# A graph network's edge loop: twelve groups of edges gathered by TensorE instead of seven, in a PSUM bank of their own, and two of VectorE's one-hot builds merged

## The chip, the cores and the metric

One NeuronCore of a Trainium2 chip. The metric is the device time of one launch in microseconds. Before the change it is 1136.53 us, the median of three runs (1135.17 to 1138.17).

## The reference

3125 nodes with 128 features, 100000 edges sorted by destination, float32. Two graph layers, each followed by a residual sum and a layer norm:

```python
# layer 0, on x
msgs = z[edge_dst] @ Wd + z[edge_src] @ Ws + edge_weight[:, None] * ww[None, :] + bm
agg = segment_max(msgs, edge_dst)            # 0 for nodes without an edge
out = relu(z @ W1a + agg @ W1b + b1) @ W2 + b2
x = layernorm(x + out)
# layer 1, on x, twice (128 -> 256 with relu, 256 -> 128)
mean = segment_sum(x[src], dst) / max(deg, 1)
h = mean @ Wl.T + bl + x @ Wr.T
x = layernorm(x + h2)
```

The term `z[edge_src] @ Ws` is a gather of rows from the table zs = x @ Ws, which is written to memory once (`zs_d`).

## The kernel before

**Groups and slots.** The edges are cut into 196 groups of 512 (two superbatches of 256). All engines step through the same numbered slots k, each with its own order written out by hand in a loop `for k in range(SLOTS)`, and meet by semaphores. In slot k, TensorE (PE) first does the halves of `pieces` that fall there, then `rows_T(k)` (the messages of group k, transposed into `T_BANK`: one matmul for the edge weights, L1614, and four transposes of gathered rows, L1626), `adjacent(k-2)` (L1675, L1678: counts of edges per source tile and destination column; L1685: the running maxima at the ends of segments), `products(k-1)` (four transposes of the scan, L1665), the matmuls of a node tile if one is due, `degree`, and last the `pick_rows` of this slot. VectorE (DVE) does `scan(k)` (L1225), `pick(k-1)` (L1217), `one_hots(k-1)` (L1208 to L1210), the steps of a node tile, degree rows and their reciprocal (L1244, L1249), and `make_hot` for the next slot (L1303). ScalarE (ACT) does `cast_hot` (L909), `adjacent` (L863, L864: counts copied into `adj`, maxima into `aggT`), `messages` (L869) and copies for the node tiles. SyncE (SP) loads the mask row and the weights of group k (`load_edges`, L502, L505), stores tiles and scale rows, and loads `parts_d` quads; its queue is in order, and it waits on semaphores in it.

**Gathers.** GpSimd (POOL) issues four indirect DMAs for each group (L1037), 128 rows of 128 floats each, into the ring `gring`, which has places for GR = 4 groups. For group g it waits until `rows_T(g-4)` is done (`t_ps`). Five groups (`OWN`: 38, 70, 102, 134, 166) take their last 128 rows by plain DMAs of SP, so POOL has three gathers there.

**Picked groups.** POOL skips the groups in `PICKED`. Their rows are gathered by PE: for each of the 25 node tiles, `make_hot` on DVE compares 512 source numbers with the tile's 128 node numbers (128x512, float16 in, bfloat16 out), `cast_hot` on ACT turns that into fp32r, and `pick_rows` multiplies it by the high and the low half of the table's tile (two matmuls with 512 columns, L1785). `PICKS` pairs each picked group with the slot at which this begins: (17, 7), (28, 17), (37, 28), (48, 37), (60, 50), (80, 71), (93, 85). The 25 tiles are spread evenly over those slots (`hots`). The sums are kept in `L_BANK` until `rows_T` of that group adds the edge weights.

**What else is in L_BANK.** The first layer-1 sums (`pieces`, L1748, planned by `plan()`: from slot 49 on, 12 matmuls with 512 columns over two slots each, then more of them) and the degree rows (`degree`, L1706, slots 61 to 65, 93 to 97, 125 to 129 and later). So picks are placed between them, and each waits for the other with `scanned(picked_before(...))` and `acc_sb`, `deg_sb`.

**Node tiles.** Tile t (128 nodes) is complete at slot `turn(t)` = 8t + 9. Its x is transposed into bank `M1` at slot turn + 1, `values` follows at + 3, `hidden` (DVE, L1258) at + 4, `outputs` at + 5, `stats`, root and `normed` at + 6 to + 8, and `roots` and `copy_zr` at + 12 and + 13.

After the loop (from about 981 us) follow the rest of layer 1 and the second aggregation as a product with the count matrix; the change does not touch them, but for the steps of the last two node tiles.

Of the kernel before, what the change touches and what calls it, by code (L numbers as in the profile page):

```python
# [4 lines left out]
P = 128  # L5
# [17 lines left out]
HR = 4  # L23
# [26 lines left out]
PICKS = ((17, 7), (28, 17), (37, 28), (48, 37), (60, 50), (80, 71), (93, 85))  # L50
# [3 lines left out]
HOTS = 4  # L54
ROW = AW // 2
SPARE = 801
# [70 lines left out]


def picked_before(k):
    return max([g for g in PICKED if g < k], default=-1)  # L130
# [10 lines left out]
def gnn_kernel(nc, x, src, dst, w, Wm, bm, W1, b1, W2, b2, W1lT, b1l, W1rT, W2lT, b2l, W2rT, out):  # L141
# [19 lines left out]
    with ctx:  # L161
# [69 lines left out]
        def spare(row, n, lead=0):  # L231
            return slice(row * ROW + SPARE + lead, row * ROW + SPARE + lead + n)

        key_i = adj_w[:, spare(0, 512)].bitcast(i32)
        key_w = adj_w[:, spare(1, 512)]
        keys = [adj_w[:, spare(2, 256, 256 * i)].bitcast(f16) for i in range(2)]
        hot_b = [adj_w[:, spare(3 + i // 2, 256, 256 * (i % 2))].bitcast(bf16) for i in range(HOTS)]
        hot_r = [nc.alloc_sbuf_tensor_at(f"hot_r{i}", [P, 512], f32r, offset=adj_at + 32 * ((ROW * (5 + i) + SPARE) // 8))[:, :]
                 for i in range(HOTS)]

# [13 lines left out]
        raw_l = raw_w.rearrange("p (a b) -> p a b", b=512)  # L254
        quads = quad, raw_w[:, 0:6 * F].bitcast(bf16).rearrange("p (a b) -> p a b", b=3 * F)
# [79 lines left out]
        T_BANK, S_BANK, L_BANK, A_BANK, M0, M1 = bank[0:2], bank[2], bank[3], bank[4:6], bank[6], bank[7]  # L335
# [113 lines left out]
        def _(sp):  # L449
# [65 lines left out]
            def usual():  # L515
# [47 lines left out]
                def load_key(i):  # L563
                    g = PICKED[i]
                    if i:
                        sp.wait_ge(key_float, i)
                    sp.dma_start(key_i, src[512 * g:512 * g + 512].rearrange("(o e) -> o e", o=1).broadcast_to([P, 512])).then_inc(l_key, 16)
# [214 lines left out]
        def _(act):  # L782
# [67 lines left out]
            def usual():  # L850
# [20 lines left out]
                def copy_xr(t):  # L871
                    act.wait_ge(xr_ps, t + 1)
                    if t:
                        act.wait_ge(v_ps, t)
                    nc.scalar.copy(xTt[:, 0:size(t)], M1[:, P:P + size(t)]).then_inc(xr_sb, 1)
# [10 lines left out]

                def copy_zr(t):
                    act.wait_ge(zr_ps, t + 1)
                    for a in range(2):
                        last = nc.scalar.activation(zr_of(t)[:, a, 0:size(t)], M1[:, (2 + a) * P:(2 + a) * P + size(t)], ACT.Identity, bias=b1l_c[:, a:a + 1])  # L890
                    last.then_inc(zr_sb, 1)
# [6 lines left out]
                def key_to_float(i):  # L898
                    act.wait_ge(l_key, 16 * (i + 1))
                    if i:  # L900
                        act.wait_ge(keyed, i)
                    nc.scalar.copy(key_w, key_i).then_inc(key_float, 1)

                def cast_hot(i, h):
# [4 lines left out]
                    nc.scalar.copy(hot_r[u % HOTS], hot_b[u % HOTS]).then_inc(hot_cast, 1)  # L909

                for k in range(SLOTS):
# [14 lines left out]
                    for t in tiles(k, 13, -1):  # L926
                        copy_zr(t)
                    for t in tiles(k, 10):
                        copy_x1T(t)
                    for t in tiles(k, 7):  # L930
# [171 lines left out]
        def _(dve):  # L1102
# [98 lines left out]
            def usual():  # L1201
                def one_hots(g):
                    for s in supers(g):
                        if s >= HR:
                            dve.wait_ge(ae_ps, s - HR + 2)
                        r = s % HR
                        for u in range(2):
                            nc.vector.tensor_scalar(hot_l[:, r, u, :], i_key[:, 0:P], lo_n[:, u, s:s + 1], None, ALU.is_equal)  # L1208
                            nc.vector.tensor_scalar(hot_d[:, r, u, :], i_key[:, 0:COLS], key_n[:, u, s:s + 1], None, ALU.is_equal)  # L1209
                        nc.vector.tensor_scalar(hot_x[:, r, 0:NT], i_hi[:, 0:NT], key2_n[:, s:s + 1], None, ALU.is_equal).then_inc(made, 1)  # L1210
# [8 lines left out]
                def scan(g):  # L1219
# [5 lines left out]
                    nc.vector.tensor_tensor_scan(S[:, g % 2, 0:n], mask[:, g % MR, 0:n], (L_BANK if g in PICKED else T_BANK[g % 2])[:, 0:n],  # L1225
# [24 lines left out]

                def hidden(t):
                    k = size(t)
                    dve.wait_ge(v_ps, t + 1)
                    if 0 < t < NT - 1:
                        dve.wait_ge(x1_st, 32 * t)
                        dve.wait_ge(parts_sb, t)
                        dve.wait_ge(x1T_sb, t)
                    nc.vector.tensor_scalar(hid(t)[:, 0:k], M0[:, 0:k], c0_c, 0.0, ALU.add, ALU.max).then_inc(hid_sb, 1)  # L1258
# [35 lines left out]
                def key_of(i):  # L1294
                    dve.wait_ge(key_float, i + 1)
                    nc.vector.tensor_scalar(keys[i % 2], key_w, float(CENTER), None, ALU.subtract).then_inc(keyed, 1)

                def make_hot(i, h):
                    u = NT * i + h
                    dve.wait_ge(keyed, i + 1)  # L1300
                    if u >= HOTS:
                        dve.wait_ge(hot_cast, u - HOTS + 1)
                    nc.vector.tensor_scalar(hot_b[u % HOTS], keys[i % 2], node_c[:, h:h + 1], None, ALU.is_equal).then_inc(hot_made, 1)  # L1303

                for k in range(SLOTS):
# [14 lines left out]
                    for t in tiles(k, 4):  # L1320
                        hidden(t)
# [234 lines left out]
        def _(pe):  # L1556
# [51 lines left out]
            def rows_T(g):  # L1608
                n, o = edges(g), T_BANK[g % 2]
                pe.wait_ge(l_wp[g % WR], 16 * (g // WR + 1))  # L1610
                if g in PICKED:
                    nc.tensor.matmul(L_BANK[:, :], ww9[0:9, :], wp9[:, g % WR, 0:n], start=False, stop=True).then_inc(t_ps, 1)
# [47 lines left out]
            def usual():  # L1660
# [29 lines left out]
                def x_turned(t):  # L1690
# [4 lines left out]
                    if t >= 2:  # L1695
                        pe.wait_ge(zr_sb, t - 1)
# [299 lines left out]
```

## Time and profile before

| | before |
|---|---|
| median of 3 runs | 1136.53 us |
| profiled execution, its own time | 1136.4 us |
| its span | 1134.6 us |
| PE busy | 997.1 us (88%) |
| DVE busy | 894.9 us (79%) |
| ACT busy | 500.8 us (44%) |
| POOL busy | 757.0 us (67%) |
| mean granted TensorE clock | 0.958 |

Busy time counts each instruction's record from its start to its end. Records of neighbouring instructions on PE and DVE overlap, since these engines are pipelined: what an instruction costs its engine is the distance from its start to the next one's start, which is shorter than its record.

### The profile page before, as it was taken

What the parts mean: (1) busy time and instruction counts of PE and PEld (TensorE: products, weight loads), DVE (VectorE), ACT (ScalarE), POOL (GpSimd) and SP (SyncE); (2) the same over time, 40 slices, a digit from 0 to 9 for tenths busy, and PEclk for the clock granted to TensorE, in tenths of its full rate; (3) what the DMA queues carried; (4) which work ended last, traced back from release to release, by engine and by line L of the source; (5) the groups of instructions that cost most, each with busy time, mean ns of one, the idle gap of its engine ahead of it and who ended that gap; (6) DMA issues with size and microseconds to landing.
All of it is one profiled execution on the core that took longest, in us unless ns stands there. A gap on an engine that the chain in (4) does not pass through costs nothing.

```text
span 1134.6 us, 23462 instructions
## 1 busy us (share of the span) xinstructions
PE 997.1 (88%) x6407; PEld 735.8 (65%) x6449; DVE 894.9 (79%) x3127; ACT 500.8 (44%) x1434; POOL 757.0 (67%) x802
## 2 busy tenths in 40 slices
PE   4689999999997999978797879886889899899997
PEld 4367767767765777756665656565556577656776
DVE  6488999999886999897777778777788788746455
ACT  3256766666542656533333323333324233312664
POOL 6657777777777777777777777777777777200332
PEclk9789999999997999989898889999999999999999
DMA  8724344344344343334434334433344354446221
GB/s 210 214 61 94 92 98 109 94 99 114 89 97 106 91 119 97 91 85 127 110 87 93 90 97 129 105 91 89 87 132 110 106 150 97 117 134 177 83 58 42
DMA packets 123128, 121.14 MB, mean 107 GB/s; under 512 B 24307, under 2 KB 106392, under 8 KB 122989
## 3 DMA queue, kind: packets, MB, share of 16 engines
q1 hardware_dynamic: 95920, 69.21, 22.7%
q0 software_dynamic: 23968, 49.13, 18.0%
q10 hardware_dynamic: 3101, 1.21, 0.4%
q8 instruction: 54, 0.88, 0.3%
q14 instruction: 85, 0.70, 0.2%
HBM read 105.60 MB, written 13.88 MB: 105 GB/s over the span
## 4 chain that ended last, share of the span: by engine, by line
PE 36%; POOL 30%; issue 15%; DVE 12%; DMA 3%; SPq 2%; ACT 1%; ACTq 1%; DVEq 0%
POOL area L1037 30%; PE bank L1910 7%; PE bank L1748 5%; PE bank L1685 5%; PE bank L1675 3%; PE bank L1626 3%; PE bank L1785 3%; DVE area L1225 2%; DVE area L1209 2%; PE bank L1665 2%; PE bank L1875 2%; DVE area L1208 2%; PE bank L1614 2%; PE bank L1861 1%; PE bank L1706 1%
## 5 line engine op out<-in xcount | busy, mean ns | idle before, releaser
L1037 POOL DMA_INDIRECT area<-zs_d,area x729 | 705.4, 968 | 234.8 <-issue 219.3
L863 ACT CAST adj_w<-bank 128x325 f32 x391 | 176.2, 451 | 472.5 <-PE bank L1685 415.1
L1225 DVE TENSOR_TENSOR_SCAN area<-area,bank 128x512 f32<-128x512 bf16 x196 | 249.7, 1274 | 144.1 <-PE bank L1626 126.5
L1209 DVE TENSOR_SCALAR area<-area 128x325 bf16<-128x325 f16 x782 | 249.5, 319 | 0.0
L1685 PE MATMUL bank<-area 128*128 128x104 f32 x1564 | 234.0, 294 | 0.1
L1208 DVE TENSOR_SCALAR area<-area 128x128 bf16<-128x128 f16 x782 | 212.1, 271 | 0.0
L1685 PEld LDWEIGHTS bank<-area 128*128 128x128 f32 x1564 | 204.7, 204 | 11.3 <-ACT area L869 1.9
L1675 PE MATMUL bank<-area 128*128 128x325 bf16 x782 | 157.2, 316 | 22.0 <-DVE area L1210 15.8
L1626 PE MATMUL bank<-ident,area 128*128 128x128 f32 x734 | 123.1, 291 | 45.8 <-DMA area<-zs_d,area 45.4
L1626 PEld LDWEIGHTS bank<-ident,area 128*128 128x128 f32 x734 | 78.1, 142 | 91.1 <-DMA area<-zs_d,area 57.2
L1748 PE MATMUL bank<-adj_w,area 128*128 128x512 bf16 (+5 forms) x497 | 108.5, 357 | 24.6 <-DMA area<-parts_d 8.6
L1665 PE MATMUL bank<-ident,area 128*128 128x128 f32 x782 | 121.0, 278 | 0.0
L869 ACT COPY area<-bank 128x512 f32<-128x512 f32 x196 | 118.3, 604 | 4.7 <-issue 3.3
L909 ACT CAST hot_r<-adj_w 128x512 fp32r<-128x512 bf16 x175 | 98.0, 622 | 48.3 <-DVE adj_w L1303 47.5
L1058 POOL CAST counts<-adj_w 128x512 fp32r<-128x512 bf16 (+2 forms) x45 | 28.2, 631 | 124.1 <-DVE area L1357 74.7
L1785 PE MATMUL bank<-hot_r,zs_r 128*128 128x512 f32 (+1 forms) x350 | 99.7, 414 | 0.4 <-issue 0.3
L1210 DVE TENSOR_SCALAR area<-area 128x25 bf16<-128x25 bf16 x391 | 97.4, 249 | 0.0
L1665 PEld LDWEIGHTS bank<-ident,area 128*128 128x128 f32 x782 | 96.1, 151 | 0.3 <-issue 0.3
L1614 PE MATMUL bank<-area,ww 9*128 9x512 bf16 x189 | 74.4, 394 | 20.9 <-DMA area<-wp_d 20.8
L1675 PEld LDWEIGHTS bank<-area 128*128 128x128 bf16 x782 | 61.6, 100 | 45.9 <-DVE area L1210 22.9
L1748 PEld LDWEIGHTS bank<-adj_w,area 128*128 128x128 bf16 (+1 forms) x525 | 48.6, 98 | 64.3 <-issue 21.4
L1678 PE MATMUL bank<-area 128*128 128x25 bf16 x390 | 74.5, 191 | 0.0
(174 smaller groups left out, 1067.6 us busy)
## 6 DMA issues: line engine op xcount, KB each, us to landing
area<-mask_d SPq DMA_DIRECT2D x195, 128.0 KB
area<-zs_d,area POOLq DMA_INDIRECT x729
area<-zs_d SPq DMA_DIRECT2D x640, 0.5 KB
area<-parts_d SPq DMA_DIRECT2D x20, 384.0 KB, 7.6
area<-wp_d SPq DMA_DIRECT2D x195, 9.0 KB
zr_d<-area SPq DMA_DIRECT2D x24, 128.0 KB
area<-zr_d SPq DMA_DIRECT2D x6, 512.0 KB, 4.5
area<-scale_d SPq DMA_DIRECT2D x11, 256.0 KB, 4.3
```

What stands on the lines that cost most here:

```text
L863: nc.scalar.copy(adj[:, :, bass.ds(at, W)], A_BANK[s % 2][:, 0:COLS].rearrange("p (h w) -> p h w", w=W))
L869: nc.scalar.copy(St[:, 0:n], S_BANK[:, 0:n]).then_inc(st_sb, 1)
L1037: pool.indirect_dma_start(gring[:, g % GR * 4 + s % 2 * 2 + u, :], None, x if g < RAW else zs_d[0:N, :], bass.IndirectOffsetOnAxis(ap=firs ...
L1208: nc.vector.tensor_scalar(hot_l[:, r, u, :], i_key[:, 0:P], lo_n[:, u, s:s + 1], None, ALU.is_equal)
L1209: nc.vector.tensor_scalar(hot_d[:, r, u, :], i_key[:, 0:COLS], key_n[:, u, s:s + 1], None, ALU.is_equal)
L1225: nc.vector.tensor_tensor_scan(S[:, g % 2, 0:n], mask[:, g % MR, 0:n], (L_BANK if g in PICKED else T_BANK[g % 2])[:, 0:n], S[:, (g + 1) % ...
L1626: last = nc.tensor.matmul(o[:, b * P:(b + 1) * P], rows, ident[:, :], start=False, stop=b == n // P - 1, is_transpose=True)
L1665: last = nc.tensor.transpose(S_BANK[:, b * P:(b + 1) * P], S[:, g % 2, b * P:(b + 1) * P], ident[:, :])
L1675: last = nc.tensor.matmul(o[:, 0:COLS], hot_l[:, r, u, :], hot_d[:, r, u, :], start=u == 0, stop=u == 1 and s == 0)
L1685: last = nc.tensor.matmul(o[:, 384:384 + WIDE * W].rearrange("p (n w) -> p n w", w=W), St[:, b * P:(b + 1) * P], sel[:, g % 2, u, s % 2, : ...
L1748: last = nc.tensor.matmul(o[:, 0:b - a], row[0:k, i * F:(i + 1) * F], adj[0:k, h, a:b], start=start and i == 0, stop=stop and i == 2)
L1785: last = nc.tensor.matmul(L_BANK[:, :], part_of[0:n, h - SPLITS[at][1], :], hot_r[u % HOTS][0:n, :], start=h == 0 and part_of is zs_high[a ...
```

## The change

`PICKS` becomes twelve groups over slots 20 to 145, end to end. They get bank 7 (`G_BANK`) for themselves, and the waits between picks, pieces and degrees go. The node tiles' x and root products move from that bank into `M0`, `roots` and `copy_zr` come a slot earlier, and `hidden` moves from DVE to ACT (`hidden_of`). On DVE, the four 128x128 one-hots of a group become one `tensor_tensor` and the two 128x25 ones another. The buffers of the picks move (`hot_r`, the keys: four runs of 128 words in rows of `adj`, `hot_b`: three buffers in `aggT`).

```diff
-PICKS = ((17, 7), (28, 17), (37, 28), (48, 37), (60, 50), (80, 71), (93, 85))
+PICKS = ((30, 20), (40, 30), (51, 40), (61, 51), (72, 61), (82, 72), (93, 82), (103, 93), (114, 103), (124, 114), (135, 124),
+         (145, 135))
...
-        hot_b = [adj_w[:, spare(3 + i // 2, 256, 256 * (i % 2))].bitcast(bf16) for i in range(HOTS)]
+        hot_r = [nc.alloc_sbuf_tensor_at(f"hot_r{i}", [P, 4 * ROW], f32r, offset=adj_at + 32 * ((ROW * (8 + 4 * i) + SPARE) // 8))[:, :]
+                 .rearrange("p (h n) -> p h n", n=ROW)[:, :, 0:P] for i in range(HOTS)]
+        hot_b = [aggT[:, FREE + 256 * i:FREE + 256 * i + 256].bitcast(bf16) for i in range(RAWS)]
...
+        def x_bank(t):
+            return (M0 if t < NT - 2 else G_BANK)[:, P:2 * P]
+        def root_bank(t):
+            return M0[:, P:3 * P] if t < NT - 2 else G_BANK[:, 2 * P:4 * P]
...
+                def hidden_of(t):
+                    k = size(t)
+                    act.wait_ge(v_ps, t + 1)
+                    if 0 < t < NT - 1:
+                        act.wait_ge(x1_st, 32 * t)
+                        act.wait_ge(parts_sb, t)
+                        act.wait_ge(x1T_sb, t)
+                    nc.scalar.activation(hid(t)[:, 0:k], M0[:, 0:k], ACT.Relu, bias=c0_c).then_inc(hid_sb, 1)
...
                 def one_hots(g):
-                    for s in supers(g):
-                        if s >= HR:
-                            dve.wait_ge(ae_ps, s - HR + 2)
-                        r = s % HR
-                        for u in range(2):
-                            nc.vector.tensor_scalar(hot_l[:, r, u, :], i_key[:, 0:P], lo_n[:, u, s:s + 1], None, ALU.is_equal)
-                            nc.vector.tensor_scalar(hot_d[:, r, u, :], i_key[:, 0:COLS], key_n[:, u, s:s + 1], None, ALU.is_equal)
-                        nc.vector.tensor_scalar(hot_x[:, r, 0:NT], i_hi[:, 0:NT], key2_n[:, s:s + 1], None, ALU.is_equal).then_inc(made, 1)
+                    s, m = 2 * g, len(supers(g))
+                    r = s % HR
+                    if s >= HR:
+                        dve.wait_ge(ae_ps, min(s + m, NS) - HR + 1)
+                    low = lo_n[:, :, s:s + m].unsqueeze(3).broadcast_to([P, 2, m, P])
+                    count = i_key[:, 0:P].unsqueeze(1).unsqueeze(1).broadcast_to([P, 2, m, P])
+                    nc.vector.tensor_tensor(hot_l[:, r:r + m, :, :].rearrange("p s u e -> p u s e"), count, low, ALU.is_equal)
+                    for n in range(m):
                         for u in range(2):
+                            nc.vector.tensor_scalar(hot_d[:, r + n, u, :], i_key[:, 0:COLS], key_n[:, u, s + n:s + n + 1], None, ALU.is_equal)
+                    carried = key2_n[:, s:s + m].unsqueeze(2).broadcast_to([P, m, NT])
+                    tiles_at = i_hi[:, 0:NT].unsqueeze(1).broadcast_to([P, m, NT])
+                    nc.vector.tensor_tensor(hot_x[:, r:r + m, 0:NT], tiles_at, carried, ALU.is_equal).then_inc(made, m)
...
                 def pick_rows(i, h):
                     u, n = NT * i + h, size(h)
                     if h == 0:
-                        g, a = PICKS[i]
                         pe.wait_ge(zs_low_sb, len(SPLITS))
-                        pe.wait_ge(raw_sb, RAW)
                         if i:
                             pe.wait_ge(scanned, PICKED[i - 1] + 1)
-                        before = len([p for p in PIECES if p[0] < a])
-                        if before:
-                            pe.wait_ge(acc_sb, before)
-                        rows = len([d for d in DEGREE_SLOTS if d < a])
-                        if rows:
-                            pe.wait_ge(deg_sb, rows)
                     pe.wait_ge(hot_cast, u + 1)
                     at = [b for b, (_, h0, h1) in enumerate(SPLITS) if h0 <= h < h1][0]
                     for part_of in (zs_high[at], zs_low[at]):
-                        last = nc.tensor.matmul(L_BANK[:, :], part_of[0:n, h - SPLITS[at][1], :], hot_r[u % HOTS][0:n, :],
+                        last = nc.tensor.matmul(G_BANK.rearrange("p (a e) -> p a e", e=P), part_of[0:n, h - SPLITS[at][1], :], hot_r[u % HOTS][0:n],
                                                 start=h == 0 and part_of is zs_high[at], stop=False)
                     last.then_inc(hot_used, 1)
```

## Rows read from the trace of the kernel before

**Rows 1.** The page: the chain that ended last, by engine and by line.
```profile
PE 36%; POOL 30%; issue 15%; DVE 12%; DMA 3%; SPq 2%; ACT 1%; ACTq 1%; DVEq 0%
```

**Rows 2.** Waits, whole span: who waited for whom, us in total, times, longest.
```profile
POOL area L1037 <- PE bank L1626: 14.6, 16, 8.6
```

**Rows 3.** POOL's groups of instructions: xcount | busy, mean ns | idle before; 170.8:259.9, then 727.8:816.5.
```profile
L1037 POOL DMA_INDIRECT area<-zs_d,area x69 | 68.6, 995 | 21.0 <-issue 20.1 <-PE bank L1626 0.9
...
L1037 POOL DMA_INDIRECT area<-zs_d,area x71 | 68.1, 959 | 21.6 <-issue 21.6
```

**Rows 4.** Waits of PE in 540:640, a stretch without picks.
```profile
PE bank L1626 <- DMA area<-zs_d,area: 16.6, 12, 2.4
```

**Rows 5.** Busy time by stretch: us, PE, PEld, DVE, ACT, POOL, PEclk, DMA share, GB/s.
```profile
76.60:259.90 183.30, 175.87 (x1186) 133.29 (x1185) 172.07 (x643) 122.62 (x330) 140.57 (x141) 0.99 0.40 98
```

**Rows 6.** The scans L1225 alone, by stretch (x50 is groups 0 to 49).
```profile
0.00:264.01 264.01, 62.43 (x50) 0.96 0.48 120
264.01:727.81 463.80, 122.61 (x96) 0.94 0.41 101
```

**Rows 7.** The gathers L1037 alone, up to the scan of group 49.
```profile
3.80:264.01 260.21, 189.27 (x188) 0.96 0.48 121
```

**Rows 8.** PE in order of time, one slot with picks: start, us, line, xcount.
```profile
250.68 0.38 PE L1614 MATMUL bank<-area,ww 9*128 9x512 bf16 x1
...
252.10 1.12 PE L1685 MATMUL bank<-area 128*128 128x104 f32 x8
...
253.49 0.39 PE L1725 MATMUL bank<-w,area 128*128 128x128 f32 x2
253.63 1.18 PE L1785 MATMUL bank<-hot_r,zs_r 128*128 128x512 f32 x4
254.75 0.39 PE L1614 MATMUL bank<-area,ww 9*128 9x512 bf16 x1
```

**Rows 9.** PE in order of time, stretches 136:138 and 351:372.
```profile
136.77 1.32 PE L1785 MATMUL bank<-hot_r,zs_r 128*128 128x512 f32 x5
...
351.94 0.38 PE L1614 MATMUL bank<-area,ww 9*128 9x512 bf16 x1 [2.13 <-DMA area<-wp_d]
...
364.58 2.34 PE L1748 MATMUL bank<-adj_w,area 128*128 128x512 bf16 x5 [4.22 <-DMA area<-parts_d]
...
371.15 1.46 PE L1748 MATMUL bank<-adj_w,area 128*128 128x512 bf16 x6
```

**Rows 10.** DVE in order of time, 251:255 and 345:349.
```profile
251.69 1.28 DVE L1225 TENSOR_TENSOR_SCAN area<-area,bank 128x512 f32<-128x512 bf16 x1
252.89 0.19 DVE L1217 TENSOR_TENSOR area<-area 128x52 f32<-128x52 bf16 x1
...
253.80 0.23 DVE L1210 TENSOR_SCALAR area<-area 128x25 bf16<-128x25 bf16 x1
253.94 0.24 DVE L1208 TENSOR_SCALAR area<-area 128x128 bf16<-128x128 f16 x1
254.10 0.30 DVE L1209 TENSOR_SCALAR area<-area 128x325 bf16<-128x325 f16 x1
...
345.20 3.34 DVE L1249 RECIPROCAL area<-area 1x512 f32<-1x512 f32 x1
```

**Rows 11.** Groups by shape: the nearest operations to the new ones.
```profile
L1394 DVE TENSOR_TENSOR area<-area 128x512 f32<-128x512 f32 x5 | 3.4, 684 | 2.4 <-DMA area<-r_d 2.4
...
L890 ACT ACTIVATE area<-bank,cols 128x128 f32<-128x128 f32 x48 | 15.6, 390 | 1.6 <-PE bank L1742 1.6
```

**Rows 12.** POOL and DVE in order of time, about 137.9 and about 201.7.
```profile
137.73 0.61 DVE L1303 TENSOR_SCALAR adj_w<-adj_w,node_c 128x512 bf16<-128x512 f16 x2
137.91 1.24 POOL L1037 DMA_INDIRECT area<-zs_d,area  x1 [0.30 <-issue]
...
201.57 0.94 POOL L1037 DMA_INDIRECT area<-zs_d,area  x1 [0.30 <-PE bank L1626]
...
201.96 0.29 DVE L1287 TENSOR_TENSOR area<-area 128x128 bf16<-128x128 f32 x1
```

More of the change, by code:

```diff
@@ L229, in gnn_kernel, with spare @@
         zs_low = [z[:, :, low_at:ROW] for z in zs_r]
[L231 to L236, printed above, removed]
-        hot_b = [adj_w[:, spare(3 + i // 2, 256, 256 * (i % 2))].bitcast(bf16) for i in range(HOTS)]
-        hot_r = [nc.alloc_sbuf_tensor_at(f"hot_r{i}", [P, 512], f32r, offset=adj_at + 32 * ((ROW * (5 + i) + SPARE) // 8))[:, :]
-                 for i in range(HOTS)]
+        def spare(row, rows):
+            return adj_w.rearrange("p (h n) -> p h n", n=ROW)[:, row:row + rows, SPARE:SPARE + P]
+        key_w = spare(0, 4)
+        key_i = key_w.bitcast(i32)
+        keys = [spare(4 + 2 * i, 2).bitcast(f16) for i in range(2)]
+        hot_r = [nc.alloc_sbuf_tensor_at(f"hot_r{i}", [P, 4 * ROW], f32r, offset=adj_at + 32 * ((ROW * (8 + 4 * i) + SPARE) // 8))[:, :]
+                 .rearrange("p (h n) -> p h n", n=ROW)[:, :, 0:P] for i in range(HOTS)]
         AREA = 15776
@@ L889, in copy_zr @@
                     for a in range(2):
-                        last = nc.scalar.activation(zr_of(t)[:, a, 0:size(t)], M1[:, (2 + a) * P:(2 + a) * P + size(t)], ACT.Identity, bias=b1l_c[:, a:a + 1])
+                        last = nc.scalar.activation(zr_of(t)[:, a, 0:size(t)], root_bank(t)[:, a * P:a * P + size(t)], ACT.Identity, bias=b1l_c[:, a:a + 1])
                     last.then_inc(zr_sb, 1)
@@ L925, in usual @@
                             key_to_float(i)
-                    for t in tiles(k, 13, -1):
+                    for t in tiles(k, 12):
                         copy_zr(t)
@@ L929, in usual @@
                         copy_x1T(t)
+                    for t in tiles(k, 4):
+                        hidden_of(t)
                     for t in tiles(k, 7):
@@ L1611, in rows_T @@
                 if g in PICKED:
[L1612 removed]
+                    nc.tensor.matmul(G_BANK[:, :], ww9[0:9, :], wp9[:, g % WR, 0:n], start=False, stop=True).then_inc(t_ps, 1)
                     return
@@ L1741, in roots @@
                     for a in range(2):
-                        last = nc.tensor.matmul(M1[:, (2 + a) * P:(2 + a) * P + k], w1r[:, a * P:(a + 1) * P], zr_of(t)[:, 0, 0:k], start=True, stop=True)
+                        last = nc.tensor.matmul(root_bank(t)[:, a * P:a * P + k], w1r[:, a * P:(a + 1) * P], zr_of(t)[:, 0, 0:k], start=True, stop=True)
                     last.then_inc(zr_ps, 1)
@@ L1821, in usual @@
                         products(k - 1)
-                    for t in tiles(k, 12, -1):
+                    for t in tiles(k, 11):
                         roots(t)
```

51 lines of the change are left out of this document (21 added, 30 removed).

## The prediction, written before the changed kernel was run

> **What bounds the kernel now.** I read the page first. Its chain splits the span between PE and POOL [rows 1]: neither view alone says what a change is worth. The waits come next: the pace of the loop is POOL's. POOL waited for PE 14.6 us in all, 8.6 of them at once in the start-up [rows 2]; otherwise it issued gather after gather, and what it sat idle before each is its own issue time of 0.3 us. So one gather costs (68.1 + 21.6)/71 = 1.26 us where nothing is picked, and (68.6 + 21.0)/69 = 1.30 us where picks run [rows 3]. In a stretch without picks PE waits for the rows to land [rows 4]. With four gathers a slot that is 5.04 us a slot, and a picked group costs POOL nothing.
>
> Where picks run it is different. From the scan of group 7 to that of group 48, 41 slots take 183.3 us, 4.47 a slot, with PE 175.9 us busy and DVE 172.1 [rows 5]. All three engines are near their end there. What the change is worth is therefore PE's work in the slots 49 to 145, where picks now run beside pieces and degrees.
>
> **What POOL is spared.** Twelve picked groups in place of seven: 5 x 4 = 20 gathers, at 1.26 to 1.30 us 25 to 26 us. No group of `OWN` is picked. If only POOL counted, that would be the gain.
>
> **What PE has to do in a slot.** A slot with two of the 25 node tiles of a pick goes from 250.68 to 254.75, 4.07 us [rows 8]. A matmul of a pick costs (1.32 - 0.41)/4 = 0.23 us from start to start (five in a run, the last counted with its record of about 0.41) [rows 9]. The two of L1725 go from 253.49 to 253.63, and by the next ones' distance I take 0.11 each for any 128-column float32 matmul of a node tile. So the bare slot is 4.07 - 4 x 0.23 - 2 x 0.11 = 2.93 us. A matmul of a piece costs (1.46 - 0.38)/5 = 0.216 [rows 9]; a degree's has the same shape.
>
> From slot 49 to slot 145 (96 slots) after the change, on PE:
> - 96 x 2.93 = 281.3
> - 12 node tiles x 12 small matmuls x 0.11 = 15.8
> - 230 pick tiles (50 + 77 + 75 + 28 by `hots`) x 2 x 0.232 = 106.7
> - 12 pieces x 12 x 0.216 = 31.1, and 75 degree matmuls x 0.216 = 16.2
> - less 9 picked groups x 4 transposes x 0.11 = -4.0
>
> Sum 447.1 us. POOL has 341 gathers in these slots, 430 to 443 us. So PE becomes the bound there, if narrowly.
>
> **What PE loses on top.** In rows 5 I can size what the sum leaves out: 41 x 2.93 + 100 x 0.464 + 5 x 1.32 - 4 x 0.44 = 171.4 of 183.3 us, 0.29 us a slot. There DVE was as full as PE, and a node tile's steps on DVE held PE up. After the change DVE has less in each slot. The merged 128x128 one-hots: the nearest rows are L1394, a tensor_tensor with 512 float32 elements, 0.684 us [rows 11], less the 0.08 by which a record overlaps the next start (the scan: 1.28 long, 1.20 to the next) [rows 10], 0.60 us, against 4 x 0.16 = 0.64 for the four. From below it could be no longer than one 128x325 instruction (0.3); from above 0.68; I take 0.60, since `lo_n` is float32 as in L1394. The merged 128x25 has 50 elements: at most the 0.16 of one L1208 with 128, against 2 x 0.14 for L1210 [rows 10]. `hidden` leaves too, 0.26 us in eight slots. Together 0.19 us a slot less, while PE's slot grows from 4.2 to 4.65; so DVE is no longer beside PE, and I take nothing for the steady slots. The new single wait of `one_hots` (for the first superbatch of group g-1 instead of the second one of g-2) costs nothing: PE's fourth L1685 of the slot ends at about 252.10 + 3 x 0.12 + 0.28 = 252.74 [rows 8], before DVE's pick has begun at 252.89 [rows 10]. Its price if PE is late: 0.5 us a slot for DVE, which has that.
>
> What does not go away is the three reciprocals of degree rows, 3.34 us each on DVE [rows 10], at slots 66, 98 and 130, now all in slots full of picks. The scan behind one is late by that, PE waits for it, and SP, which waits for the row too, loads the next weights late: the 2.13 us before L1614; the quad behind it costs 4.22 us more [rows 9]. Before, these waits fell where PE had 1 us to spare a slot. Now PE arrives later at each (1.1 us a slot), which hides most of the quad and the weights, but not the scan. I take 3.3 us each, 10 in all; bounds: 0, and 3 x (3.34 + 2.13 + 4.22) = 29.
>
> Does the merged instruction hold POOL up? A gather beside the picks' 128x512 one-hots lasts 1.24 us instead of 0.94, but one beside L1287, a tensor_tensor with both operands in SBUF, 0.94 [rows 12], so I take nothing for it. The Trainium skill ("SBUF — State Buffer", Who interferes with whom) speaks against the change here: a DVE instruction with two SBUF inputs contends with a GpSimd instruction that reads SBUF, and L1287 is four times shorter than the new one. By the row the sum stays; by the rule the merge has a price, which is rival 4.
>
> **The path.** At slot 49 there have been two picks instead of four by then: POOL is 8 gathers further back, 8 x 1.28 = 10.2 us. PE was behind POOL there: 188 gathers issued where 183 were needed [rows 7], 5 against 3 where POOL bounds, so 2.5 us are won back. Slot 49 comes at 264.0 + 7.7 = 271.7 us. Slot 145 comes at 271.7 + 447.1 + 10 = 728.8, against 727.8 before [rows 6]: no gain up to there. But POOL has run ahead meanwhile. The ring holds at most three groups and the one just freed, 12 gathers, or 8 where a picked group is among them, against 3 now: 5 to 9 gathers, 6 to 11 us; I take 9. PE can make it up in the 17 slots from 145 to 162, 17 x 3.1 + 48 x 0.216 + 25 x 0.216 = 68 us of work in 88.7 us (727.8 to 816.5) [rows 3]. From 162 on nothing changes. The gain is 9 - 1 = 8 us. Against the profiled execution, 1136.4 us (its span 1134.6 and 1.8 around it; the median is 1136.5), that gives 1128.4.
>
> The smaller edits: `hidden_of` puts a 0.39 us activation on ACT [rows 11] every eighth slot, where ACT is busy 122.6 of 183.3 us [rows 5]; if ACT were full it would cost 25 x 0.39 = 10 us. The picks read in four runs of 128 cost PE nothing: L1685 reads runs of 13 without showing it. If each run went like a matmul of its own (0.11), 230 x 2 x 0.21 = 97 us would come on top; I hold that end for unlikely. The tail after 981 us keeps its order; `hidden` on ACT there costs 0.05 us a tile.
>
> **The rivals.**
> 1. POOL stays the bound everywhere (chance 0.15). For it: PE's sum is only 4 to 17 us over POOL's, and the ring covers 9 of that. Against it: the reciprocals. Then the 20 gathers count in full, less 125 more pick tiles that stretch some gathers: 17 to 25 us, 1115.
> 2. The gain is eaten up (0.16): PE loses 0.18 us a slot more than I take and the result is within 0.3% (3.4 us), 1136. I call 0.3% what this kernel's measurement can just tell from no change.
> 3. PE is the bound and stays as loosely coupled as in rows 5 (0.27): 0.29 us lost a slot over 96 slots is 28 us in place of 10. Then slot 145 comes 19 us late, the ring gives 9 back, 1136.4 + 10 = 1146. The point from which this decides: more than 18 us lost in slots 49 to 145. For it: this is the only measured value of such slots. Against it: there DVE had as much work as PE, and now it has 0.19 us a slot less, and PE 0.45 more.
> 4. The merged instruction holds POOL up (0.04). If each merged one-hot stretched one gather by the 0.3 us that the picks' one-hots cost one [rows 12], in the 100 slots where POOL bounds that is 30 us, less the 8: 1158.
>
> **How the numbers follow.** My forecast, a gain of 4 to 17 us with PE the bound in the picks' stretch, has 0.38; the rivals 0.15, 0.16, 0.27 and 0.04. Faster by over 0.3%: 0.38 + 0.15 = 0.53; within 0.16; slower 0.27 + 0.04 = 0.31. The range, 1114 to 1148, takes in rivals 1 to 3 without their outer ends; the forecast's own is 1120 to 1132.
>
> **What would show it.** Count the scans: slot 49 about 8 us later than before, slot 145 about level, slot 162 about 8 us earlier. In the stretch between 49 and 145 POOL should wait for PE's L1626 or L1614 by 10 to 25 us in all, where now it waits for nothing; rival 1 has no such wait. L1785 should still last about 0.41 us and cost 0.23. The 128x128 one-hot should show x196 at about 0.69 us. PE's granted clock should stay at 2.4 GHz from 49 to 145. I am wrong if slot 145 comes over 10 us later than before, or if PE waits for DVE between the reciprocals.

## The result and the profile after

The changed kernel is slower: 1151.76 us, the median of four runs (1148.52 to 1154.53), against 1136.3 before (the median of four runs, one more than stood above). The ratio is 1.0118, interval 1.0084 to 1.0151. The prediction was 1128.4, within 1114 to 1148; both the sign and the range were wrong. The profiled execution took 1153.4 us, 17.0 more than that of before.

The page of the changed kernel: span, busy times, and the chain by engine, to be read against rows 1.

```profile
span 1151.6 us, 23629 instructions
...
PE 1051.9 (91%) x6637; PEld 772.5 (67%) x6679; DVE 875.2 (76%) x2451; ACT 578.7 (50%) x1589; POOL 752.9 (65%) x782
...
PE 49%; POOL 24%; issue 11%; DVE 8%; DMA 4%; SPq 2%; ACTq 1%; ACT 1%; DVEq 0%
```

PE's share of the chain went from 36% to 49%, POOL's from 30% to 24%: the bound moved as forecast. How much was lost with it shows in the scans (L1225 is now L1244), by stretch.

```profile
0.00:271.00 271.00, 62.57 (x49) 0.92 0.46 118
271.00:750.30 479.30, 122.58 (x96) 0.98 0.38 99
750.30:828.20 77.90, 21.73 (x17) 1.00 0.39 95
```

The cut points are the scans of groups 49, 145 and 162 after the change. Group 49 comes at 271.0 us, 7.0 later than before [rows 6]; I had 7.7. Group 145 comes at 750.3, against 727.8: 22.5 later, where I had 1.0. From 145 to 162 it takes 77.9 us instead of 88.7, so the ring gives 10.8 back; I had 9. Most of the miss is in the middle: 479.3 us against 463.8 before, and against my sum of 447.1 + 10. The slots from 162 to 195 add 3.9 us (168.2 against 164.3), where I expected nothing. The profiled execution is 25.0 us over the forecast: 22.2 of them fall in the middle stretch, 3.9 in the slots from 162, 1.4 after the loop, less 0.7 up to slot 49 and 1.8 in the ring.

All engines in the last two of these stretches (the length in us, PE, PEld, DVE, ACT, POOL, granted clock, DMA share, GB/s).

```profile
271.00:750.30 479.30, 461.03 (x2971) 336.51 (x2991) 400.58 (x1143) 288.37 (x789) 344.81 (x350) 0.98 0.38 99
750.30:828.20 77.90, 69.14 (x484) 48.90 (x491) 59.04 (x163) 28.45 (x97) 59.43 (x61) 1.00 0.39 95
```

POOL's gathers in the middle one, by groups.

```profile
L1051 POOL DMA_INDIRECT area<-zs_d,area x350 | 345.6, 987 | 134.8 <-issue 100.9 <-PE bank L1636 32.9 <-PE bank L1622 1.0
```

PE's longest waits in the same stretch (us in total, times, longest).

```profile
PE bank L1787 <- ACT hot_r L921: 5.3, 3, 1.9
PE bank L1636 <- DMA area<-zs_d,area: 3.5, 3, 1.8
PE bank L1685 <- ACT area L869: 2.2, 4, 0.9
PE bank L1624 <- DMA area<-wp_d: 1.9, 4, 0.8
PE bank L1759 <- DMA area<-parts_d: 1.5, 1, 1.5
...
PE bank L1685 <- DVE area L1229: 0.4, 1, 0.4
```

PE is busy 461.0 of 479.3 us and bounds the stretch. The last line is its wait for the one-hots that VectorE builds for each group: hardly any. POOL waits 33.9 us for it there (1.2 before), 44.0 in the whole span against the 14.6 of rows 2. That is the wait that I named as the mark of a PE bound, and it is larger than the 10 to 25 us I gave it. Note also the mean gather: 987 ns with 350 of them, where before it was 962 in the same stretch.

Now one degree row's reciprocal, that of slot 66 (line L1268). DVE, PE and SP of the changed kernel, each in order of time.

```profile
357.74 0.19 DVE L1229 TENSOR_TENSOR area<-area 128x50 bf16<-128x50 bf16 x1
...
359.01 3.34 DVE L1268 RECIPROCAL area<-area 1x512 f32<-1x512 f32 x1
362.39 0.72 DVE L1314 TENSOR_SCALAR area<-adj_w,node_c 128x512 bf16<-128x512 f16 x2
363.03 1.27 DVE L1244 TENSOR_TENSOR_SCAN area<-area,bank 128x512 f32<-128x512 bf16 x1
...
367.64 1.28 DVE L1244 TENSOR_TENSOR_SCAN area<-area,bank 128x512 f32<-128x512 bf16 x1 [0.72 <-PE bank L1636]
...
374.58 1.28 DVE L1244 TENSOR_TENSOR_SCAN area<-area,bank 128x512 f32<-128x512 bf16 x1 [2.58 <-PE bank L1636]
```

```profile
361.04 0.60 PE L1675 MATMUL bank<-ident,area 128*128 128x128 f32 x4
363.56 1.64 PE L1787 MATMUL bank<-hot_r,zs_r 128*128 128x512 f32 x4 [1.92 <-ACT hot_r L921]
365.95 0.60 PE L1624 MATMUL bank<-area,ww 9*128 9x512 bf16 x1 [0.75 <-DMA area<-wp_d]
...
368.60 2.01 PE L1695 MATMUL bank<-area 128*128 128x104 f32 x8
```

```profile
362.38 0.23 SPq L534 DMA_DIRECT2D scale_d<-area  x1
362.65 0.36 SPq L506 DMA_DIRECT2D area<-mask_d  x1
363.06 0.34 SPq L509 DMA_DIRECT2D area<-wp_d  x1
```

The reciprocal holds DVE for 3.34 us, from 359.01 to 362.35. `make_hot` (L1314) and the scan stand behind it, so PE first misses its one-hots (1.92 us). SP stands behind it too: the scale row's store waits for the reciprocal, and the weights `wp_d` for slot 68 are issued only at 363.06, so PE misses them as well (0.75 us). After these stalls PE is slow: L1624 takes 0.60 us instead of 0.38 and L1695 2.01 instead of 1.12 (L1614 and L1685 of [rows 8]). The granted clock shows why (us, PE, granted clock, DMA share, GB/s), first in three windows about this place, then in the three pieces of the whole stretch from 49 to 145 in which it was low.

```profile
357.90:365.90 8.00, 5.13 (x28) 0.89 0.38 86
365.90:370.30 4.40, 4.34 (x19) 0.50 0.44 118
370.30:373.50 3.20, 3.20 (x20) 0.88 0.18 58
```

```profile
323.30:326.70 3.40, 3.40 (x19) 0.50 0.36 94
364.20:371.00 6.80, 6.05 (x25) 0.50 0.51 126
521.30:528.00 6.70, 6.36 (x27) 0.50 0.24 63
```

From 364.2 to 371.0 us the granted clock was 0.50, 1.2 GHz. It fell just after PE had stood idle for 1.92 us; in the 8.00 us to 365.9 PE was busy 5.13. The second reciprocal (slot 98) is followed by the same, from 521.3 to 528.0; behind the third (slot 130) the clock stays at 1.00. The piece at 323.3 has no reciprocal: PE had just waited 1.78 us for gathered rows. Busy time grows in such a piece without more work being done: a view of busy shares hides this loss, and the window's clock shows it.

That adds up for the three reciprocals. PE's waits behind them are 5.3 us for one-hots (the first line of its waits above) and 1.9 for weights (the fourth), and 13.5 us at half the clock lose 6.8 more: 14.0 us.

### The profile page after: what moved, and what is told of

It is laid out like the page before. It is cut to its first block, busy times and chain, and to the rows that moved or that the text cites. A ratio compares the mean times of both kernels' runs of the same rounds, so it can differ in the third digit from the quotient of the medians.

```text
span 1151.6 us, 23629 instructions
## 1 busy us (share of the span) xinstructions
PE 1051.9 (91%) x6637; PEld 772.5 (67%) x6679; DVE 875.2 (76%) x2451; ACT 578.7 (50%) x1589; POOL 752.9 (65%) x782
## 4 chain that ended last, share of the span: by engine, by line
PE 49%; POOL 24%; issue 11%; DVE 8%; DMA 4%; SPq 2%; ACTq 1%; ACT 1%; DVEq 0%
POOL area L1051 24%; PE bank L1695 8%; PE bank L1787 7%; PE bank L1912 6%; PE bank L1759 6%; PE bank L1685 4%; PE bank L1636 4%; PE bank L1675 3%; PE bank L1624 2%; PE bank L1716 2%; PE bank L1877 2%; DVE area L1226 2%; DVE area L1244 1%; DMA area<-zs_d,area 1%; DMA area<-wp_d 1%
## 5 line engine op out<-in xcount | busy, mean ns | idle before, releaser
L1244 DVE TENSOR_TENSOR_SCAN area<-area,bank 128x512 f32<-128x512 bf16 x196 | 249.8, 1275 | 167.1 <-PE bank L1636 138.3
L1695 PE MATMUL bank<-area 128*128 128x104 f32 x1564 | 230.2, 291 | 0.1
L1695 PEld LDWEIGHTS bank<-area 128*128 128x128 f32 x1564 | 200.6, 201 | 11.0 <-ACT area L874 2.1
L921 ACT CAST hot_r<-area 128x512 fp32r<-128x512 bf16 x300 | 169.9, 626 | 75.6 <-DVE area L1314 73.5
L1226 DVE TENSOR_SCALAR area<-area 128x325 bf16<-128x325 f16 x782 | 190.0, 307 | 0.0
L1787 PE MATMUL bank<-hot_r,zs_r 128*128 128x512 f32 x600 | 177.7, 423 | 6.2 <-ACT hot_r L921 5.3
L1685 PE MATMUL bank<-area 128*128 128x325 bf16 x782 | 153.5, 311 | 11.7 <-DVE area L1229 7.9
L1223 DVE TENSOR_TENSOR area<-area 128x512 bf16<-128x512 f16 x196 | 134.3, 685 | 9.0 <-PE bank L1695 8.3
L1787 PEld LDWEIGHTS bank<-hot_r,zs_r 128*128 128x128 f32 x600 | 103.7, 190 | 30.5 <-ACT hot_r L921 7.2
L1759 PE MATMUL bank<-adj_w,area 128*128 128x512 bf16 (+5 forms) x497 | 108.2, 357 | 15.6 <-DVE area L1256 7.8
L1314 DVE TENSOR_SCALAR area<-adj_w,node_c 128x512 bf16<-128x512 f16 x300 | 94.4, 363 | 0.2
L1685 PEld LDWEIGHTS bank<-area 128*128 128x128 bf16 x782 | 61.0, 99 | 35.0 <-DVE area L1229 11.7
L1624 PE MATMUL bank<-area,ww 9*128 9x512 bf16 (+1 forms) x184 | 72.3, 393 | 11.3 <-DMA area<-wp_d 11.1
```

What stands on the lines that cost most here:

```text
L921: nc.scalar.copy(hot_r[u % HOTS], hot_b[u % RAWS].rearrange("p (a e) -> p a e", e=P)).then_inc(hot_cast, 1)
L1223: nc.vector.tensor_tensor(hot_l[:, r:r + m, :, :].rearrange("p s u e -> p u s e"), count, low, ALU.is_equal)
L1226: nc.vector.tensor_scalar(hot_d[:, r + n, u, :], i_key[:, 0:COLS], key_n[:, u, s + n:s + n + 1], None, ALU.is_equal)
L1685: last = nc.tensor.matmul(o[:, 0:COLS], hot_l[:, r, u, :], hot_d[:, r, u, :], start=u == 0, stop=u == 1 and s == 0)
L1695: last = nc.tensor.matmul(o[:, 384:384 + WIDE * W].rearrange("p (n w) -> p n w", w=W), St[:, b * P:(b + 1) * P], sel[:, g % 2, u, s % 2, : ...
L1759: last = nc.tensor.matmul(o[:, 0:b - a], row[0:k, i * F:(i + 1) * F], adj[0:k, h, a:b], start=start and i == 0, stop=stop and i == 2)
```

## The experiments

Ratios are to the kernel before, on the same chip, with 95% intervals. The expectations name their theories by letters. **A:** PE is the bound, and the whole reciprocals cost it far more than 3.3 us each. **B:** PE loses its time a little in every slot. **C:** the merged one-hots, the bank `M0` or `hidden` on ACT cost the time. Later, where seven picks were slow too, C was split: **D**, the merged one-hots stretch POOL's gathers (D1 by the long instruction itself, D2 by the order or the wait that come with it, D3 by the wait alone), and **E**, the rest of the change does it. Times of different experiments can come from different chips; the ratios are what is compared.

**The reciprocals in four parts.** The first four degree rows' reciprocals are cut into quarters of 128 elements, one a slot; the row is stored three slots later.

```diff
-                    row = scale_row(j)
-                    nc.vector.reciprocal(row, row).then_inc(scale_sb, 1)
+                    n = (span(j)[1] - span(j)[0]) // parts if parts > 1 else span(j)[1] - span(j)[0]
+                    row = scale_row(j)[:, q * n:(q + 1) * n]
+                    last = nc.vector.reciprocal(row, row)
+                    if q == parts - 1:
+                        last.then_inc(scale_sb, 1)
```

> The changed kernel with the reciprocal of each of the first four degree rows in four parts of 128, one a slot, and its store three slots later. Theory A (the single 3.34 us reciprocals hold PE up in the dense slots 66, 98 and 130, directly, through the one-hots behind them on VectorE and through SP's late loads, about 6.5 us each): slot 145 comes 12 to 20 us earlier than in the changed kernel (750), the time is 1133 to 1141. Theory B (PE loses its time a little in every slot): slot 145 stays within 5 us, 1147 to 1152.

Measured: 1133.16 us, 0.9954 [0.9934, 0.9974], so 18.6 us less than the changed kernel (the ratios, 1.0118 and 0.9954, give as much). DVE of this kernel in order of time, in two neighbouring slots.

```profile
357.94 0.94 DVE L1271 RECIPROCAL area<-area 1x128 f32<-1x128 f32 x1
358.90 0.65 DVE L1319 TENSOR_SCALAR area<-adj_w,node_c 128x512 bf16<-128x512 f16 x2
359.47 1.27 DVE L1246 TENSOR_TENSOR_SCAN area<-area,bank 128x512 f32<-128x512 bf16 x1
...
362.53 0.94 DVE L1271 RECIPROCAL area<-area 1x128 f32<-1x128 f32 x1
```

All engines in its stretch from group 49 to 145, and then the largest wait of PE and POOL's wait for PE in it.

```profile
274.40:734.30 459.90, 453.20 (x2972) 331.09 (x2991) 402.45 (x1153) 287.49 (x789) 344.20 (x348) 1.00 0.40 103
```

```profile
PE bank L1692 <- ACT area L871: 2.3, 4, 1.0
...
POOL area L1053 <- PE bank L1643: 12.7, 10, 3.6
```

The stretch takes 459.9 us instead of 479.3. The three pieces that hold a reciprocal give 15.2 of the 19.4: scans 66 to 71 take 24.8 us instead of 30.3, 98 to 103 24.8 instead of 30.2, 130 to 135 24.7 instead of 29.0. So a whole reciprocal costs 5.1 us more than one in four parts, where I had 3.3 in all. The other 4.2 lie in slots 49 to 61 (53.9 for 58.4), where the changed kernel's PE had waited 1.78 us for gathered rows and then run 3.4 us at the granted clock of 0.50; no reciprocal is there. Seen by busy time, 7.8 of the 19.4 us are the same matmuls taking longer (461.0 against 453.2, x2971 and x2972) and 11.6 are idle time. The clock is 1.00 in the whole stretch.

The fourth reciprocal that was cut, in slot 162, gives nothing that stays: it lies where POOL bounds. The changed kernel does take 3.8 us more from scan 180 to 195 (73.8 for 70.0), but its reciprocal there, in slot 189, is whole in both kernels. PE had waited 2.6 us for gathered rows at 958.6 and ran at a granted clock of 0.61, then 0.70, up to 967; the kernel with the reciprocals behind `make_hot` (below) takes 68.7 us there. So this is a stall of one execution.

Theory A holds for what the split gives back. Of the 32.2 us over my sum of PE's work, 12.8 are still there (459.9 - 447.1), spread over the 96 slots: that much of B is true as well.

**The same split in the kernel before.** The same edit, with seven picks and the old one-hots.

> The kernel before with only the reciprocals in four parts. POOL bounds it nearly everywhere and has room for a late slot, so by theory A nothing is gained: ratio 0.996 to 1.002. If TensorE's lost time counted there too: 0.990 or less.

Measured: 1135.66 us, 0.998 [0.9959, 1.0001]. Where POOL bounds, the reciprocals cost about 2 us, by the interval between nothing and 4.7: their price is that of a full PE. In the profiles, scans 66 to 71 do take 32.6 us before and 23.2 with the split, and yet slot 145 comes no sooner (727.8 and 732.5): what is lost there is made good in the slots behind it.

**Reciprocal behind `make_hot`.** The changed kernel with the two calls exchanged, so that the next slot's one-hots don't wait for the reciprocal, but the scan and SP still do.

```diff
-                    if k - 1 in DEGREE_SLOTS[:6]:
-                        scale_from(DEGREE_SLOTS.index(k - 1))
...
+                    if k - 1 in DEGREE_SLOTS[:6]:
+                        scale_from(DEGREE_SLOTS.index(k - 1))
```

> The changed kernel with the whole 3.34 us reciprocal, but behind make_hot instead of ahead of it. If a reciprocal costs its 6.5 us mostly by holding up the next slot's one-hots (TensorE's wait for ScalarE's cast, 1.9 us, then its half clock): 3 us less each, 1142 to 1146. If by the late scan and SP's late loads: as the changed kernel, 1149 to 1153.

Measured: 1149.67 us, 1.0123 [1.0092, 1.0154], no different from the changed kernel's 1.0118. In its profile a whole reciprocal costs as much as ever: scans 66 to 71, 98 to 103 and 130 to 135 take 29.8, 29.8 and 29.9 us, 5.0 each over the split. The wait has only moved. PE no longer waits for its one-hots, but behind each of the three for the weights of the next slot but one, 3.3 to 3.5 us; the first time SP issued them at 358.47, right behind the scale row's store. After each such wait the granted clock is 0.50 for 3.4 us. PE's wait for weights from slot 49 to 145:

```profile
PE bank L1624 <- DMA area<-wp_d: 10.2, 3, 3.5
```

So SP's late loads are what PE waits for last in this kernel. The late scan stands close behind them: VectorE ends the 128x325 one-hots that follow the scan at about 360.7, and PE needs them some 0.8 us after the start at 360.87. From that I estimate that weights in time alone would give back about 1 us of the 3.4; no run has tried it.

**The picks undone.** The changed kernel with the seven `PICKS` of before; banks, `hidden` on ACT, buffers and merged one-hots stay.

```diff
-PICKS = ((30, 20), (40, 30), (51, 40), (61, 51), (72, 61), (82, 72), (93, 82), (103, 93), (114, 103), (124, 114), (135, 124),
-         (145, 135))
+PICKS = ((17, 7), (28, 17), (37, 28), (48, 37), (60, 50), (80, 71), (93, 85))
```

> The changed kernel with the seven picks of before at their slots of before, everything else of the change kept. Theory A and B both (the loss comes from the placement of twelve picks, slots 49 to 145): POOL bounds again, 1133 to 1138. Rival C (the merged one-hots, the M0 bank or hidden on ScalarE cost the time): 1145 or more, with gathers longer than in before.

Measured: 1147.15 us, 1.0073 [1.0042, 1.0103]. Slower than before with not one gather more: something else in the change costs some 8 us where POOL bounds. The 1133 to 1138 us that A and B had in common are missed, and C's condition is met.

**Picks and one-hots undone.** As the last one, with `one_hots` of before too: ten `tensor_scalar` and two waits. It ran twice.

```diff
-                    nc.vector.tensor_tensor(hot_l[:, r:r + m, :, :].rearrange("p s u e -> p u s e"), count, low, ALU.is_equal)
...
+                            nc.vector.tensor_scalar(hot_l[:, r, u, :], i_key[:, 0:P], lo_n[:, u, s:s + 1], None, ALU.is_equal)
+                            nc.vector.tensor_scalar(hot_d[:, r, u, :], i_key[:, 0:COLS], key_n[:, u, s:s + 1], None, ALU.is_equal)
+                        nc.vector.tensor_scalar(hot_x[:, r, 0:NT], i_hi[:, 0:NT], key2_n[:, s:s + 1], None, ALU.is_equal).then_inc(made, 1)
```

> e2 (seven picks) with one_hots of before. Theory D (the merged one-hots stretch POOL's gathers: 1.278 against 1.259 us from gather to gather between groups 102 and 162): gathers there back at 1.26, slot 162 back to 817 us, ratio to before 0.997 to 1.003. Theory E (M0 bank, hidden on ScalarE, the strided buffers cost e2's 0.7%): ratio 1.005 or more.

> e5 once more, beside e13 and e14 on one chip, as their base: 0.998 to 1.002.

Measured: 1139.26 us, 0.9995 [0.9974, 1.0017], and 1138.78, 1.0015 [0.9991, 1.0038]. So undoing the one-hots gives back 7 to 9 us, and `M0`, `hidden` on ACT, the four runs of the picks' reads and the moved buffers cost nothing that is clear of these intervals. The gathers from the scan of group 102 to that of 162, a stretch without picks: first with the merged one-hots, then with the old ones.

```profile
L1050 POOL DMA_INDIRECT area<-zs_d,area x240 | 233.5, 973 | 73.2 <-issue 72.9 <-PE bank L1635 0.3
```

```profile
L1050 POOL DMA_INDIRECT area<-zs_d,area x237 | 226.6, 956 | 72.2 <-issue 71.6 <-PE bank L1630 0.6
```

The mean gather grows by 17 ns. By the 729 gathers of table rows that is 12.4 us, against 0.6 to 0.8% measured, 7 to 9 us. The mean hides that most gathers are untouched and a few are much longer: 27 of 240 are over 1 us (mean 1186 ns), against 17 of 237 (mean 1055). What VectorE was doing when a gather began tells them apart. With merged one-hots, 25 gathers began during the merged 128x512 instruction, and these took 1190 ns in the mean; 22 of the 27 long ones are among them. The 86 that began while VectorE was idle took 943. With the old one-hots, those that began during a 128x128 or 128x325 instruction took 970 to 1000. One of the 25, DVE and POOL together, in the kernel with merged one-hots:

```profile
645.09 0.68 DVE L1222 TENSOR_TENSOR area<-area 128x512 bf16<-128x512 f16 x1
645.19 1.40 POOL L1050 DMA_INDIRECT area<-zs_d,area  x1 [0.30 <-issue]
```

The gather began 0.10 us after the merged instruction and took 1.40 us instead of 0.94: 0.46 more, while 0.58 of that instruction lay ahead. The Trainium skill ("SBUF — State Buffer", Who interferes with whom) says that a `tensor_tensor` with two SBUF inputs contends with GpSimd's reads; this trace agrees, by the 1190 ns against 943. The same section infers that such an instruction does not hold up descriptor generation, and an indirect DMA held up in this way speaks against that.

**Only the 128x128 one-hots merged**, the 128x25 ones separate, seven picks.

```diff
+                        nc.vector.tensor_scalar(hot_x[:, r + n, 0:NT], i_hi[:, 0:NT], key2_n[:, s + n:s + n + 1], None, ALU.is_equal).then_inc(made, 1)
+                    return
```

> e2 with only the four 128x128 one-hots merged, the 128x25 ones separate. Theory D with the long instruction (0.69 us, two operands in SBUF) as the cause: as e2, ratio 1.005 to 1.010. If the short merged 128x25 is what costs: as e5, 1.000 to 1.003.

Measured: 1147.97 us, 1.0097 [1.0068, 1.0126]; mean gather 969 ns. Undoing the small merge alone gains nothing.

**The old instructions in the new order.** Seven picks; four 128x128, four 128x325, two 128x25, all `tensor_scalar`, with the single wait; then the same with the two waits of before; then the old order with the single wait.

```diff
+                    for n in range(m):
+                        for u in range(2):
+                            nc.vector.tensor_scalar(hot_l[:, r + n, u, :], i_key[:, 0:P], lo_n[:, u, s + n:s + n + 1], None, ALU.is_equal)
...
```

> e2 (seven picks) with separate one-hots again, but in the order and with the single wait of the merged ones: four 128x128, then four 128x325, then two 128x25. Theory D1 (the long tensor_tensor itself holds gathers up): ratio as e5, 0.997 to 1.003, gathers 1.26 us apart. Theory D2 (the four 128x325 in a row, or the single wait, do it): as e8, 1.007 or more.

> e9 (all 128x128 first, then all 128x325) with the two waits of before. If the order costs (D2, four 128x325 in a row hold POOL's gathers): ratio 1.005 to 1.010, gathers longer than in e5. If e9 lost by its wait: 0.998 to 1.002.

> e5 (seven picks, one_hots of before) with the single, later wait of the merged version ahead of the first superbatch. If the wait costs (D3): ratio 1.005 or more, with VectorE waiting for TensorE's L1695-like matmuls before its one-hots. If not: as e16, 0.998 to 1.002.

Measured: new order 1145.76 us, 1.0084 [1.0054, 1.0113]; with two waits 1143.63, 1.0057 [1.0032, 1.0082]; old order with the single wait 1136.77, 0.9997 [0.9972, 1.0022]. The wait costs nothing, as I had said. The order costs 0.4% with two waits (against the old order's 1.0015 with two, on the same chip: 4.9 us) and 0.9% with the single one (against 0.9997); the 0.997 to 1.003 that D1 had for the new order are missed. The intervals of the new orders and of the merged one overlap, so much of what I had put down to the long instruction may be that instructions of one kind now stand in a row. The gathers from 102 to 162 with the new order and two waits, then with the old order and one:

```profile
L1050 POOL DMA_INDIRECT area<-zs_d,area x237 | 228.3, 963 | 72.3 <-issue 72.3
```

```profile
L1050 POOL DMA_INDIRECT area<-zs_d,area x236 | 224.9, 953 | 72.0 <-issue 72.0
```

These two differ in the wait as well. Among kernels with equal waits the new order has 963 ns against 956, and 959 against 953: 6 or 7 ns a gather, by 729 gathers 4 to 5 us. That is the size of the 4.9 us measured with two waits, and half of what the single wait shows. The merged instruction has 973, but its time is no more than that of the new orders by over 0.4%. How order and length share the cost isn't settled.

**Old one-hots beside twelve picks**, without and with the split reciprocals.

> The changed kernel with one_hots of before (ten instructions a group, wait for each superbatch). Theory A or B: VectorE has 0.04 to 0.2 us more a slot, 1151 to 1156. Rival C (the merged instruction waits for TensorE or holds POOL up): 5 us or more faster than the changed kernel, 1146 or less.

> e1 (twelve picks, reciprocal in four parts) with one_hots of before. Theory D: POOL bounds e1 in slots 20 to 61 and after 150, so 70 slots gain 0.08 us each, 5 us; the dense slots lose up to 0.1 us each to VectorE: ratio 0.990 to 0.999. Theory E: no faster than e1, 0.995 or more.

Measured: 1153.97 us, 1.013 [1.0086, 1.0173], beside 1.0118 for the changed kernel; and 1134.84, 0.9977 [0.9954, 1.0], beside 0.9954. Here undoing the merge gains nothing. (With the split, D had 0.990 to 0.999 and E 0.995 or more; the result lies in both, but it is no faster than with the merge.) The first of them reaches group 49 at 268.5 us, 2.5 sooner, and then takes 487.8 us to group 145, 8.5 longer. The pair with split reciprocals shows the same: 267.7 for 274.4 us, then 468.4 for 459.9. Where PE and DVE bound, fewer DVE instructions are worth as much as they cost POOL elsewhere.

**Ten picks that begin at slot 7**, split reciprocals; merged, then old one-hots.

```diff
+PICKS = ((17, 7), (27, 17), (38, 27), (49, 38), (64, 49), (80, 66), (96, 82), (112, 98), (127, 112), (143, 130))
```

> As e1, with ten picks: (17,7), (27,17), (38,27), (49,38), (64,49), (80,66), (96,82), (112,98), (127,112), (143,130): dense where there are no pieces, sparse where there are. Theory A: PE stays under POOL's pace nearly everywhere, three picks fewer gathers of POOL than before (12 gathers, 15 us): 1119 to 1127. Theory B: 1128 to 1136.

> e4 (ten picks, reciprocal in four parts) with one_hots of before. POOL bounds e4 in most slots, so theory D gives the most here: 7 to 12 us faster than e4, ratio 0.986 to 0.991. Theory E: as e4, 0.996.

Measured: 1134.9 us, 0.9959 [0.9933, 0.9985], and 1122.53, 0.9863 [0.9819, 0.9908]. With PE no longer the bound the merge costs 1.0%; that is why the first of them missed the 1119 to 1127 us that theory A had for it. And the gathers count nearly in full: 12 fewer at 1.28 us are 15.4 us, and 1.37% of 1137 are 15.6, of which the split itself, 0.998 in the kernel before, may be 2.

**Eleven picks**, spread by PE's free time: dense in slots 7 to 49, every 13 or 14 slots after that; old and merged one-hots.

```diff
+PICKS = ((17, 7), (27, 17), (38, 27), (49, 38), (62, 49), (76, 62), (89, 76), (103, 89), (116, 103), (130, 116), (143, 130))
```

> e7 with eleven picks: (17,7), (27,17), (38,27), (49,38), (62,49), (76,62), (89,76), (103,89), (116,103), (130,116), (143,130). By the sum TensorE and POOL are level at one pick in 13.4 slots between 49 and 143 (4.66 us a slot each). If POOL still bounds: 4 gathers, 5 us less than e7, ratio 0.982. If TensorE bounds: as e7 or up to 8 us slower, 0.986 to 0.993.

> e11 with the merged one-hots. POOL bounds e11 in most slots. Theory D (merging stretches gathers by 20 to 30 ns each): 12 to 18 us slower than e11, ratio 0.995 to 1.001. If merging were only a cost at seven picks' balance: as e11, 0.985.

Measured: 1119.31 us, 0.9849 [0.9822, 0.9876], the lowest of all and faster than both kernels; merged 1127.27, 0.992 [0.9894, 0.9946], so the merge costs 8 us here, where I had expected 12 to 18. The best kernel's page (span and chain), POOL's wait for PE over the whole span, and all engines from group 49 to 145:

```profile
span 1116.5 us, 24231 instructions
...
PE 52%; DVE 15%; POOL 15%; issue 11%; DMA 3%; SPq 2%; ACTq 1%; ACT 1%; DVEq 0%
```

```profile
POOL area L1052 <- PE bank L1637: 13.1, 17, 4.9
```

```profile
264.99:715.89 450.90, 430.55 (x2874) 311.28 (x2895) 410.65 (x1479) 259.16 (x732) 341.17 (x354) 1.00 0.40 104
```

PE is busy 430.6 us there instead of 461.0, and group 49 comes at 265.0, since slots 7 to 20 are used again, where PE of the changed kernel had time (busy 64.8 of the 74.0 us from 76 to 150). The eleventh pick itself gives 0.1% over ten (0.9849 for 0.9863, well within the intervals), where its four gathers would be 0.4% if POOL alone bounded.

## Why the prediction was wrong

- **Held.** POOL's spared gathers and their price, where PE has room (the old one-hots with ten picks); slot 49 at +7.0 for +7.7; the ring's 10.8 for 9; PE as the bound; the 128x512 one-hot at 687 ns for my 0.69 us; the single wait, `hidden` on ACT, the banks and the four runs at nothing.
- **The step that failed is "What PE loses on top".** It held 10 us for the stretch from 49 to 145; 32.2 were lost (479.3 - 447.1). The kernel with split reciprocals divides them. It takes 459.9, of which PE is busy 453.2 at full clock: my sum of the work was 6.1 too low (which of its terms was short stays open), and 6.7 are small idle times in the steady slots, for which I "take nothing". The reciprocals add 15.2 where I had 10, and 4.2 fell in slots 49 to 61, at a late gather and the low clock after it.
- **Why 3.3 was too little for a reciprocal.** I counted the late scan alone, and held that PE, coming later, would hide the rest. PE was never late enough: what it missed was not the scan but its one-hots (5.3 us for the three) and the weights (1.9), and then it ran 6.8 us at the granted clock of 0.50 behind each of the first two. That the clock would stay at 2.4 GHz from 49 to 145 was wrong too: it was 0.98 in the mean. My upper bound of 29 us held. I had taken a third of it without a row of a full PE behind a reciprocal.
- **The 0.29 us a slot of rows 5.** I dropped it, since DVE has less to do after the change. Rival 3 kept it: 28 us lost, 1146. Its size came near, but its reason did not: PE waited 0.4 us for these one-hots of DVE in the stretch, not 28. With the reciprocals split, the steady slots lose 12.8/96 = 0.13 us each, neither 0.29 nor nothing.
- **The merged one-hots.** "I take nothing for it" was wrong where POOL bounds: 8 us at eleven picks, 11 at ten, 7 to 9 at seven. I priced them by L1287, a `tensor_tensor` of 0.29 us beside one gather [rows 12]; one short row was no measure for an instruction of 0.69 us that runs 196 times (L1287 has a quarter of its elements, and 0.29 us is 0.4 of its time), and of the order of the instructions I did not think at all. The Trainium skill's rule, set beside the sum as rival 4, had the right sign. The 30 us of that rival was too high by a factor of about three, as not every merged instruction meets a gather: in the 60 slots from 102 to 162, 25 gathers began during one, each 0.25 us longer, which is 0.10 us a slot for the 0.3 of the rival (an estimate from these gathers). In this kernel, though, the merge is not why it is slower: undone, 1.013.
- **The range** ended at 1148. The terms that I left at nothing or took too small all had one side: 6.1 + 6.7 + 5.2 + 4.2 = 22.2 us, against a forecast gain of 8. The 3.9 us from slot 162 on and the 1.4 behind the loop come on top; for the first, one stall of the profiled execution accounts, and the second stays open.

## What to carry to other kernels

When a change fills an engine, every stall of that engine that used to be free gets a price, and the stall's tail (a queue behind it, at times the clock after it) is part of it: look for long single instructions on the engines that feed it, and cut them up in the same step. Fill the slots where the engine had time, not an unbroken run of slots. Fewer and longer VectorE instructions save VectorE's time but can stretch GpSimd's indirect DMAs; count them by which of the two engines bounds, and undo one at a time.

## What the runs showed of the hardware that I had not expected

- An indirect DMA that begins during a two-operand VectorE instruction of 128x512 is longer: 1190 ns in the mean of 25, against 943 beside an idle VectorE; over all gathers of the stretch, 973 for 956.
- The order of the same ten `tensor_scalar` instructions moves the kernel by 0.4% with two waits and 0.9% with one; the gathers are 6 or 7 ns longer in the mean.
- From slot 49 to 145 of the changed kernel PE stood idle for 1.6 to 1.9 us at one go four times; three times the granted clock then was 0.50 for 3.4 to 6.8 us, once it stayed at 1.00.
- A reciprocal over one partition takes 3.34 us for 512 elements and 0.94 for 128: 6.25 ns an element, so cutting it costs only about 0.14 us a part.
